# Perceiver block on one core: the second context's load goes to GpSimd's queue, eight small loads go to SyncE, and VectorE's constants go ahead of the first maxima

## What is computed

```python
x = x + xattn(layernorm(x), ctx_1024, ctx_1024, Wq, bq, Wk, bk, Wv, bv, Wo, bo)   # 16 heads of 16
x = x + attn(layernorm(x), Wqkv, bqkv, Wout, bout)     # self attention over 64 rows, rotary positions
x = x + ffn(layernorm(x), wg, W, b)                    # 8 experts, one per row, with a capacity
# xattn: q, k, v = Q @ Wq.T + bq, K @ Wk.T + bk, V @ Wv.T + bv, per head
#        softmax(q @ k.T / 4) @ v, then @ Wo.T + bo
```

## Time and profile before

| what | value |
|---|---|
| median of 3 runs | 721.31 us (717.43 to 722.24) |
| the profiled execution, device time | 724.1 us |
| its span in the trace | 722.2 us |
| TensorE matmul busy | 690.0 us, 96% of the span |
| GpSimd / VectorE / ScalarE busy | 559.1 / 546.3 / 449.9 us |
| mean granted TensorE clock | 0.991 |

### The profile page before, as it was taken

The page is one execution under the profiler, slowest core; times in us unless marked ns, Lnnn a source line. Parts: engine busy times, 40 slices in busy tenths (PEclk is TensorE's granted clock), DMA queues, the critical chain, the costliest instruction groups (busy, mean ns, idle before and its releaser), DMA issues.

```text
span 722.2 us, 21609 instructions
## 1 busy us (share of the span) xinstructions
PE 690.0 (96%) x8681; PEld 516.9 (72%) x8681; DVE 546.3 (76%) x1135; ACT 449.9 (62%) x884; POOL 559.1 (77%) x378
## 2 busy tenths in 40 slices
PE   5889999999999999999999999999999998898897
PEld 2547786868776878687868786878686886666673
DVE  5498768868877887788768776877686977758766
ACT  2436765767666767676766666666666775655730
POOL 7986998899698969896989698869885798704122
PEclk9999999999999999999999999999999998999999
DMA  9586054544754354445444544444444330000212
GB/s 312 126 229 186 19 133 142 115 131 95 220 132 146 91 156 103 145 103 147 111 138 107 150 108 148 102 148 106 147 98 108 88 119 1 2 1 23 74 62 94
DMA packets 45434, 84.20 MB, mean 117 GB/s; under 512 B 8492, under 2 KB 28244, under 8 KB 45332
## 3 DMA queue, kind: packets, MB, share of 16 engines
q1 hardware_dynamic: 43720, 80.13, 40.6%
q0 software_dynamic: 912, 2.14, 1.0%
q10 hardware_dynamic: 704, 0.55, 0.3%
HBM read 36.89 MB, written 6.55 MB: 60 GB/s over the span
## 4 chain that ended last, share of the span: by engine, by line
PE 84%; POOL 5%; DVE 4%; issue 4%; DMA 1%; ACT 1%; SPq 1%; DVEq 0%; ACTq 0%; POOLq 0%
PE ps_kv L805 17%; PE ps_kv L796 16%; PE ps_out L880 13%; PE ps_score L856 12%; PE ps_front L828 11%; PE ps_score L904 2%; POOL plow L627 2%; PE ps_front L904 2%; PE ps_kv L904 2%; POOL clow L570 1%; PE ps_out L896 1%; PE ps_front L837 1%; PE ps_front L890 1%; DMA kstack<-khigh 1%; PE ps_kv L771 1%
## 5 line engine op out<-in xcount | busy, mean ns | idle before, releaser
L627 POOL TENSOR_TENSOR plow<-prob 128x1024 bf16<-128x1024 f32 (+1 forms) x201 | 377.1, 1896 | 64.4 <-ACT prob L1224 61.9
L1486 DVE TENSOR_REDUCE maxes<-ps_front 128x1 f32<-128x512 f32 (+1 forms) x416 | 268.1, 665 | 71.3 <-PE ps_front L828 69.2
L1224 ACT ACTIVATE prob<-ps_score 128x512 f32<-128x512 f32 (+1 forms) x416 | 231.3, 595 | 50.7 <-PE ps_out L880 29.3
L856 PE MATMUL ps_score<-qstack,kstack 98*128 98x128 bf16 (+1 forms) x1664 | 140.9, 220 | 0.6 <-ACT prob L1224 0.3
L856 PEld LDWEIGHTS ps_score<-qstack,kstack 98*128 98x128 bf16 (+1 forms) x1664 | 111.9, 99 | 38.6 <-ACT prob L1224 1.4
L880 PE MATMUL ps_out<-vstack,prob 128*128 128x65 bf16 (+1 forms) x1664 | 137.7, 194 | 0.7 <-DVE plow L1456 0.7
L880 PE MATMUL ps_out<-vstack,plow 128*128 128x65 bf16 (+1 forms) x1664 | 136.9, 192 | 0.0
L828 PE MATMUL ps_front<-kstack,qstack 96*128 96x512 bf16 (+1 forms) x512 | 135.7, 333 | 0.9 <-DMA kstack<-khigh 0.5
L880 PEld LDWEIGHTS ps_out<-vstack,prob 128*128 128x128 bf16 (+1 forms) x1664 | 118.6, 97 | 2.3 <-DVE plow L1456 1.0
L880 PEld LDWEIGHTS ps_out<-vstack,plow 128*128 128x128 bf16 (+1 forms) x1664 | 112.6, 98 | 3.8
L1202 ACT ACTIVATE khigh<-ps_kv,bcol 128x512 bf16<-128x512 f32 (+1 forms) x123 | 72.9, 594 | 62.8 <-PE ps_kv L796 61.8
(11 more groups left out here) (288 smaller groups left out, 869.3 us busy)
## 6 DMA issues: line engine op xcount, KB each, us to landing
kstack<-khigh SPq DMA_DIRECT2D x256, 100.1 KB, 2.2
cbuf<-in_ctxT SPq DMA_DIRECT2D x15, 1601.0 KB, 7.4
kstack<-klow SPq DMA_DIRECT2D x128, 100.1 KB, 2.2
qstack<-q_blocks SPq DMA_DIRECT2D x48, 64.0 KB, 2.4
q_blocks<-qbd SPq DMA_DIRECT2D x16, 128.0 KB, 2.0
cbuf<-in_weT SPq DMA_DIRECT2D x2, 1024.0 KB, 7.1
slot_x<-att_all SPq DMA_DIRECT2D x1, 1024.0 KB, 10.7
vstack<-slot_x SPq DMA_DIRECT2D x4, 256.0 KB, 4.7
```

Source lines behind the costliest of these rows:

```text
L627: nc.gpsimd.tensor_tensor(plow[slot][0:n, :], prob[slot][0:n, :], p_high(slot, 0, HP * P)[0:n], ALU.subtract).then_inc(plow_gps, 1)
L856: mm = nc.tensor.matmul(ps_score[0:nn, h % NSB, j * P:(j + 1) * P], kstack[par][0:98, hp, n0:n0 + nn], qstack[par][0:98, q_at(hp), :], sta ...
L1224: nc.scalar.activation(prob[slot][0:nn, e * 512:e * 512 + 512], ps_score[0:nn, h % NSB, :], ACT.Exp)\
L1486: nc.vector.reduce_max(maxes[:, hp:hp + len(unit), n], ps[:, 0:len(unit) * nn].rearrange("p (h k) -> p h k", k=nn), AX.X).then_inc(m_free, 1)
```

## The change

Three edits. (1) The load of context 1 leaves SP's list, where it stood ahead of the two loads of ones, and is issued by GpSimd after its `clow` of batch 0, on a semaphore of its own (`c_second`); readers of context 1 wait for that one. (2) The eight small loads leave GpSimd's list and are issued by SP between the queries' store and `keys(0)`. (3) The letter C moves in VectorE's list from behind the split of the second query tile to ahead of the first maximum.

```diff
 DVE_PROGRAM = [
-    ("jKBKkzkKKzKkKKzKkmmmmmmKmmjmmKCKKmmmKKmmmKmmKmKmmKmKKmmmK
...
+    ("jKBKkzkKKzKkKKzKkCmmmmmmKmmjmmKKKmmmKKmmmKmmKmKmmKmKKmmmK
...
+        def context_loaded(eng, b):
+
+            if b == 1:
+                eng.wait_ge(c_second, 16)
+            else:
+                eng.wait_ge(c_loaded[b % 2], 16 * (b // 2 + 1 - b % 2))
...
@@ block.sync
-            sp.dma_start(cbuf[1][:, :, :], ctxT[1].rearrange("(k p) n -> p k n", p=P)).then_inc(c_loaded[1], 16)
             sp.dma_start(kstack[0][96:98, :, :].rearrange("p a n -> p (a n)").bitcast(f32), ones2).then_inc(ld_ones, 16)
             sp.dma_start(kstack[1][96:98, :, :].rearrange("p a n -> p (a n)").bitcast(f32), ones2).then_inc(ld_ones2, 16)
...
             send_queries(0)
+            sp.wait_ge(ones_set, 3)
+            for r in range(3):
+                sp.dma_start(bias3[32 * r:32 * r + E, 2 * D:3 * D], be).then_inc(ld_be, 16)
+                sp.dma_start(bias3[32 * r:32 * r + 1, 0:2 * D],
+                             brows[2 * D:4 * D].rearrange("(p n) -> p n", p=1)).then_inc(ld_be, 16)
+            sp.dma_start(bvcol[:, 0, :], brows[0:D].rearrange("(k p) -> p k", p=P),
+                         allow_slow_non_contiguous=True).then_inc(ld_be, 16)
+            sp.dma_start(bvcol[:, 1, :], brows[4 * D:5 * D].rearrange("(k p) -> p k", p=P),
+                         allow_slow_non_contiguous=True).then_inc(ld_be, 16)
             for b in BATCHES:
                 keys(b)
...
@@ block.gpsimd
-                    pool.wait_ge(c_loaded[par], 16 * (b // 2 + 1))
+                    context_loaded(pool, b)
...
-            for r in range(3):
-                pool.dma_start(bias3[32 * r:32 * r + E, 2 * D:3 * D], be).then_inc(ld_be, 16)
...
-            pool.dma_start(bvcol[:, 1, :], brows[4 * D:5 * D].rearrange("(k p) -> p k", p=P),
-                           allow_slow_non_contiguous=True).then_inc(ld_be, 16)
+            pool.dma_start(cbuf[1][:, :, :], ctxT[1].rearrange("(k p) n -> p k n", p=P)).then_inc(c_second, 16)
             pool.dma_start(wqkv_sb[:, :, :], wqkv.rearrange("(k p) n -> p k n", p=P)).then_inc(ld_t, 16)
```

More of the change, by code:

```diff
@@ L131 @@
 DVE_PROGRAM = [
-    ("jKBKkzkKKzKkKKzKkmmmmmmKmmjmmKCKKmmmKKmmmKmmKmKmmKmKKmmmKmKmKmKmmKmKmmmKmmmmKmKmmmKmmKmmmmmmKmmvKKam"
+    ("jKBKkzkKKzKkKKzKkCmmmmmmKmmjmmKKKmmmKKmmmKmmKmKmmKmKKmmmKmKmKmKmmKmKmmmKmmmmKmKmmmKmmKmmmmmmKmmvKKam"
      "mKmKmmmmKmmmmKmmKmmjmmmKKmmzmKmmKkmKKmmKvKaKmmKmKmmKmKmmmmKmmmmKmmKmmmKmmKmmKmmmKKKKKvmKmmamKmmmKmmK"
@@ L385, in build @@
             sem(n) for n in ("h0_rdy", "q_sent", "w_rdy", "c_first", "kv_free_act", "v0_rdy", "v0_low"))
-        c_loaded = [sem("c_loaded0"), sem("c_loaded1")]
+        c_loaded, c_second = [sem("c_loaded0"), sem("c_loaded1")], sem("c_second")
         q_loaded = sem("q_loaded")
@@ L574, in _ @@
                 low_context(0, quarter)
-            for r in range(3):
-                pool.dma_start(bias3[32 * r:32 * r + E, 2 * D:3 * D], be).then_inc(ld_be, 16)
-                pool.dma_start(bias3[32 * r:32 * r + 1, 0:2 * D],
-                               brows[2 * D:4 * D].rearrange("(p n) -> p n", p=1)).then_inc(ld_be, 16)
-            pool.dma_start(bvcol[:, 0, :], brows[0:D].rearrange("(k p) -> p k", p=P),
-                           allow_slow_non_contiguous=True).then_inc(ld_be, 16)
-            pool.dma_start(bvcol[:, 1, :], brows[4 * D:5 * D].rearrange("(k p) -> p k", p=P),
-                           allow_slow_non_contiguous=True).then_inc(ld_be, 16)
+            pool.dma_start(cbuf[1][:, :, :], ctxT[1].rearrange("(k p) n -> p k n", p=P)).then_inc(c_second, 16)
             pool.dma_start(wqkv_sb[:, :, :], wqkv.rearrange("(k p) n -> p k n", p=P)).then_inc(ld_t, 16)
@@ L783, in project @@
                 if b or low_quarters(u) == 4:
-                    pe.wait_ge(c_loaded[par], 16 * (b // 2 + 1))
+                    context_loaded(pe, b)
                 pe.wait_ge(clow_done, 4 * b + low_quarters(u))
```

## The result

The changed kernel took 724.13 us (median of 17 runs, 719.01 to 726.03), the kernel before 721.45 (17 runs, 717.43 to 723.98): ratio 1.0034, interval 1.0019 to 1.0049. A second series of the same pair gave 1.0006 (0.9988 to 1.0024), and the kernel before measured against itself 0.9996 (0.9978 to 1.0014). So the change gives between nothing and a third of a per cent of loss; only the first series is clear of no change. Medians and ratios leave out two slow runs, one of e10 (731.18 us at a mean granted clock of 0.943) and one of before (882.45 us at 0.752). The forecast was a gain of 4.6 us, 716.7, and its range ended at 721.2: the sign was wrong, and the time lies outside. The profiled execution of after: 724.13 us, span 721.8, against 724.1 and 722.2 of before.

The account below looks back on a forecast made before the run. TensorE was taken as the bound (busy 99.89 of 100 us mid-kernel), so time won at the start is kept. 2.7 + 1.65 + 0.3 = 4.65, taken as 4.6 off the 721.3 median, gave 716.7 us; range 712.8 to 721.2.

Parts of the forecast that it names:

- GpSimd's list and `h`: Start, GpSimd: fewer issues let `h` of tile 1 end at 19.45, so TensorE's unit 6 starts 2.7 us earlier.
- The clock at 20 to 27 us: TensorE, units 6 to first maxima: without the idle stretch the granted clock stays up, saving 1.65 us.
- rival A: Start, TensorE: the clock falls anyway, so the gain is only 3.0 us, 718.3; chance 0.15.
- with no such piece left: Start, TensorE: no idle piece over two us remains, so the clock is expected to stay up, worth 1.65 us.
- SP's eight issues: SP, before the key copies: eight small issues take 4.3 us (3.7 to 6.3), hidden with 0.65 us to spare.
- Rival D: SP's list: small loads, above all two `bvcol`, cost far more than on GpSimd; slower, 723.0; chance 0.04.
- My estimate is that ... the store lands 2 to 4 us after its issue, by 19: Queries' store on SP: lands early because the loads of ones finish some 5 us earlier once context 1 has left.
- speak for my reading: DMA engines at share 0.22 from 19 us were taken as evidence that context 1 beside the store would not hold it.
- Rival B: First maxima: the store or SP's list sets them, pair 0 at 27.3 not 25.7; gain 3.0, 718.3; chance 0.17.
- Hidden, barely: VectorE's constants ahead of the first maxima: run about 23.8 to 25.9, first maximum ready at 26.1.
- The constants' 0.3 us: Old place, 39.57 us: moving VectorE's constants away brings TensorE's unit at 45.98 forward by 0.3 us; bounds 0 to 1.5.
- first two terms: Start, TensorE: 2.7 us from the earlier `h` and 1.65 us from the clock staying up.

Follow-up runs that it names:

- e10: e9 with context 1's load moved from SP's list to GpSimd's, behind its `clow` of batch 0: 723.73 us, ratio 1.0013.
- e6: e5 with VectorE's constants moved ahead of the first maxima: 723.00 us, ratio 0.9997 to the kernel before.
- e7: e5 with the five instructions of VectorE's constants spread over batch 2: 728.67 us, ratio 1.009 to the kernel before.
- e2: The changed kernel with GpSimd's issue of context 1 moved behind `h` of tile 1: 726.25 us, ratio 1.0064 to the kernel before.
- e4: The kernel before with the loads of ones and the eight small loads moved into SP's later pause: 719.32 us, ratio 0.9963.
- e9: The kernel before with small loads after batch 0's key copies, ones after context 2, GpSimd's weights after four batch-1 `clow`: 720.16 us, ratio 0.9968.
- e1: The changed kernel with VectorE's constants back at their old place: 721.89 us, ratio 1.0012 to the kernel before.
- e11: The changed kernel run again unchanged, second series and profile: 723.34 us, ratio 1.0006 to the kernel before.
- e5: e4 with GpSimd's two weight loads moved behind its batch-1 `clow`s: 719.66 us, ratio 0.9957 to the kernel before.
- e12: e9 with the five instructions of VectorE's constants spread over batch 2: 729.59 us, ratio 1.0087 to the kernel before.
- e8: The kernel before run again against itself, for a second profile: 722.58 us, ratio 0.9996.
- e3: The changed kernel with context 1 back in SP's list ahead of the ones: 726.46 us, ratio 1.0061 to the kernel before.

## Why the prediction was wrong, step by step

- **GpSimd's list and `h`: right.** The load's issue costs 0.98 (taken 0.73, bound 2.87), `h` ends at 19.03 (19.45), unit 6 follows at 20.56 (20.4). 2.55 us were won there, for 2.7. (The 0.73 to 0.79 read for an issue holds for six of the ten; the other four took 0.51 or 0.52.) The bound of 2.87 was a cost of the place in SP's list and not of the load: with the load gone, the first load of ones, 50 KB, takes 3.15 there.
- **The clock at 20 to 27 us: right in the number, with luck in the rule.** It is 1.00 from 20 to 25 us in every kernel without the `h` wait, so rival A falls. But "with no such piece left" was taken for granted: the new wait of 3.31 us made another, with the clock at 0.50 behind it. And an idle piece of this length does not always bring the fall: 1.85 and 2.26 us did, 2.63 in e6 and 3.55 in e7 (at 48 us) did not. What decides between them no run shows.
- **SP's eight issues: right.** 4.3 taken, 3.2 measured, all within SP's own wait for the store. (e2 has them too, and lands the store no later than e4 without them.) Context 1 landed at 22.5 and GpSimd waited 0.44 us for it, which cost TensorE nothing. Rival D falls: the two `bvcol` loads cost 0.39 and 0.48.
- **"My estimate is that ... the store lands 2 to 4 us after its issue, by 19": this is the step that failed.** It subtracted the ones and counted nothing for what is put beside the store. Medians from issue to landing of the two transfers of this first store, with what is on GpSimd's queue beside them: nothing 2.5 (e9), `wqkv` 4.5 (e4, e2), context 1 6.4 (e10), both 8.4 (e1, e11). In the changed kernel's own profile one of the two came early: the median is 5.4, but the later one, for which `qstack` waits, took 8.2. The two costs, 2.0 for 0.77 MB and 3.9 for 1.6 MB, add up. The rows of e9, e4, e10 and e1 in this order, then the load itself in e10, where it alone differs from e9, and a window of e10:

```profile
q_blocks<-qbd SPq DMA_DIRECT2D x2, 128.0 KB, 2.5
...
q_blocks<-qbd SPq DMA_DIRECT2D x2, 128.0 KB, 4.5
...
q_blocks<-qbd SPq DMA_DIRECT2D x2, 128.0 KB, 6.4
...
q_blocks<-qbd SPq DMA_DIRECT2D x2, 128.0 KB, 8.4
...
cbuf<-in_ctxT POOLq DMA_DIRECT2D x1, 1601.0 KB, 7.5
...
17.00:20.00 3.00, 3.00 (x20) 1.46 (x19) 2.46 (x9) 1.59 (x3) 1.85 (x3) 1.00 1.01 410
```

- At the 410 GB/s of that window the bytes of the two loads take 1.9 and 4.0 us (an estimate), which is what each cost the store. In e10 the load lands at 21.3 and the later half of the store at 21.9. So the store, 0.26 MB itself, waited for practically all of what moved beside it. A fair sharing of the bytes would have cost it no more than its own size again, about 0.6 us (also an estimate).
- The empty DMA engines of the earlier trace rows "speak for my reading", I wrote. They were empty because context 1 had been moved by then. The row described a second from which the change takes away the very reason that made it so. Rival B was the right mechanism with too small a price: its bound was "it lands as late as before", 22.5, and it landed at 23.2, with 1.1 us more in the `qstack` issues behind it. The bound had no ground; a new transfer beside it can make it later than before. First maxima: 25.7 forecast, 27.3 by B, 29.30 measured. And no rival had the low clock that such a wait can bring, 1.37 us here and 1.7 in e11.
- The Trainium skill has the rule that bears on it, in two places of DMA: Bandwidth & Descriptors. "Issuing engines are not separate DMA queues", which I weighed and set aside, and "Queues, rings and completion order": a DMA engine goes round the queues that have work, a packet of each in turn. By that, packets of a queue of long rows take their turns between those of a queue of short ones. The landings above agree in direction; that packets of the two queues really take turns is not in them, and the rule as it stands gives no price.
- **"Hidden, barely" for the constants: wrong, twice hidden.** 2.15 us were taken from where GpSimd ran other work. Ahead of the first maxima it runs `clow`, and they take 4.9 (after) to 5.9 us (e6); in e4, where GpSimd stood idle beside most of them, 1.4. In the changed kernel the late copies covered this; with copies on time it costs 3.3 us (e6 against e5), and spread over batch 2 9.4 (e12 against e9). The mask alone, e4 and then after:

```profile
36.32 0.15 DVE L1449 TENSOR_TENSOR mask<-cst 128x4 f32<-128x4 f32 x1
...
24.09 1.49 DVE L1448 TENSOR_TENSOR mask<-cst 128x4 f32<-128x4 f32 x1
```

- The prediction took the DMA rule of the Trainium skill's page SBUF — State Buffer, "SBUF: two separate sides", and passed over another of the same section: VectorE and GpSimd share a port pair as an exclusive lock, which a VectorE instruction in some modes or with two SBUF inputs needs whole. The trace agrees: 1.37 to 1.5 us for instructions that take 0.15 to 0.4 in e4, so that what is added is less than one `clow` of 1.53. The 5.36 us beside four are more than one turn, and the rule doesn't say how. That the lock is the cause is the page's word and not tested here; that the place decides is shown.
- **The constants' 0.3 us: right where it applied.** From the third maxima to the batch-1 unit it is 12.47 us in before, 12.45 in e1 and e8, and 12.11 in after and e11. But it is 12.1 in e4, e5 and e10 as well, with the constants at the old place, where they are through in 1.4 to 1.7 us: there is then nothing left to win.
- **What the sum would have been.** With the store out of the way the mechanism gives what was computed: e9 starts its first maxima at 25.48 (25.7 forecast), and e5 and e9 start their first scores at 54.9 us, against 59.0 and 58.5 in two executions of before. The lead holds: e5's last scores start at 602.6, e8's at 606.6, and their spans, both at a mean clock near 1, are 713.7 and 717.8. By their ratios e4, e5 and e9 give 2.7, 3.1 and 2.3 us. So the 4.35 of the first two terms was a fair size for the start (4.5 at the first maxima of e5 and e9), of which half to seven tenths reach the measured time.
- **The base.** I tied the forecast to the median, which is sound, but gave scatter as a random draw. It isn't quite: see below.

What isn't settled: after the first 50 us the changed kernel stands 0.3 us behind before in one pair of profiles and 1.4 in the other, yet the median of the first series is 2.7 above, that of the second 0.5. The mean granted clock of the first series' runs of after is low, 0.990, against 0.994 in the 29 runs of before beside e1 to e4 (those of before in the first series have none on record). A straight line of time over clock puts after at 722.0 us for a clock of 0.994 in the first series and 722.5 in the second, and before at 721.9 and 722.5: at the same clock no difference is left. Why the clock was lower, no run tells.

## What to carry to other kernels

A load that is taken off one queue doesn't vanish: ask where in time its bytes now move, and which short transfer on a critical path moves then; every 0.4 MB beside the store of this kernel cost it about 1 us, the time that these bytes took to move. A row that shows an idle resource is evidence for the new kernel only if what made it idle stays. And the price of a VectorE instruction is read beside the GpSimd work that it will have next to it, not where it stood before: the safest filler gap is one in which GpSimd is idle or runs short work.

## What the runs showed that I had not expected

- A VectorE cast of 72x1024 took 0.69 (before, e4), 1.58 (after), 1.97 (e6) and 5.36 us (e7, e12), by what GpSimd did beside it.
- The cost of an issue went more by its place than by the size of the load. The first issue behind `clow` takes GpSimd 0.98 us for 1.6 MB (after) and for 0.77 MB (e2, e3, e4, e9) alike, and 0.79 for 8 KB (before); the 1.6 MB at another place take 0.80 (e2). The load that stands behind those of the start in SP's list takes 2.7 to 3.2 us, be it context 1 (before, e3, e4, e5, e9) or 50 KB of ones (after, e1, e2, e11).
- A store can be held for 10 us while the DMA engines are at a mean share of 0.17 (e3).
- The scatter between runs follows the mean granted clock. Of the 29 runs of before beside e1 to e4 the one at a clock of 0.990 took 724.0 us and the one at 1.000 took 718.05; a straight line through all of them falls by 5.6 us for 0.01 of clock, and in the other kernels by 5.2 to 7.8. The profiles show one place: in before and after the window from 600 to 610 us, next to the last scores, is at 0.66, in the second executions of both (e8, e11) at 1.00, with the same waits ahead of it:

```profile
600.00:640.00 40.00, 35.14 (x380) 26.27 (x380) 28.71 (x58) 23.72 (x63) 25.98 (x32) 0.91 0.01 2
```

```profile
600.00:640.00 40.00, 34.23 (x422) 26.17 (x419) 29.35 (x61) 26.61 (x71) 25.80 (x32) 1.00 0.01 2
```

The first is after, the second the same kernel in its second series. TensorE is idle in short pieces there in both, so the clock falls in one execution and not in the other.
